# The first quad of an attention made inside the block ahead of it

## The chip, the cores and the metric

The kernel runs on one core of a Trainium2 chip. Its engines run side by side, each through its own queue in order, and wait for one another by semaphores: TensorE (PE in the profile, its weight loads PEld), VectorE (DVE), ScalarE (ACT), GpSimd (POOL) and SyncE (SP), which issues the transfers. The metric is the time of one execution on the device in microseconds (us), the median of several runs.

## The reference

The program is a stack of four layers on x, four batches of 512 tokens of width 128, each followed by a residual sum and a layer norm:

```python
x = L0_attn_x                                   # (4, 512, 128)
x = _layernorm(x + _L0_attn_ref(x, ...))        # causal attention, 16 heads
x = _layernorm(x + _L0_ffn_ref(x, ...))         # 16 experts, top 4
x = _layernorm(x + _L1_attn_ref(x, Wq, Wk, Wv)) # 16 heads of 8, no mask
x = _layernorm(x + _L1_ffn_ref(x, ...))         # two layers: local attention, gated MLP
```

The change concerns the end of the second line and the start of the third:

```python
# experts: w is the softmax of the 4 best of 16 logits
hidden = gelu(einsum('bld,efd->blef', x, w1) + b1)
exp_out = einsum('blef,edf->bled', hidden, w2) + b2
fused = sum(w[..., None] * take_along_axis(exp_out, topi[..., None], axis=2), axis=2)
# second attention; the rotation's angle depends on the batch, not on the token
q, k, v = rope(x @ Wq.T), rope(x @ Wk.T), x @ Wv.T      # 16 heads of 8
scores = einsum('bhqd,bhkd->bhqk', q, k) / sqrt(8)
out = einsum('bhqk,bhkd->bhqd', softmax(scores), v)
```

## The kernel before

The program is written by hand for each engine. It has three blocks, one behind the other: `attention0`, `experts0` and `layers`, the last holding second attention (`attention1`) and the two local layers. Between two blocks all engines meet at a barrier, and a new block's instructions begin only when all have come. Within a block nothing but the order in the code and the semaphores sets what runs when; the profile's line numbers are those of this file. Line 2754 (`cleanup_on_exit`) stands for the ends of blocks.

**Experts.** A step is one expert and one batch; 64 steps, the last four being expert 15 with batches 0 to 3. `up` (line 1040) makes the hidden products in PSUM banks 0 to 3, ScalarE applies gelu (831) and copies a high part (826), VectorE takes the low part (904), and 12 down products (1095) follow in bank 4 or 5. VectorE multiplies by the gates (977) and adds into `xT` (980). In the last steps each batch is then finished: `turn_x` transposes `xT` (1049), `copy_x` (839) puts it into `x`, `second_moments` (878, 881) and POOL's `deviation` (775, 779) give mean and deviation, `finish_norm` (910) normalises, `turn_fin` (1056) transposes back and `copy_fin` (844) writes `xT`. Batch 0's `turn_fin` stands ahead of the last 12 down products in TensorE's queue, which is strict.

**Second attention.** Its work goes by quads: 16 quads `m`, of 4 heads of one batch, 8 units each, a unit being 128 queries or keys by 2 heads. For each quad two products (`project`, 1508: w = 0 query, w = 1 key) are made; ScalarE copies a scaled leading part (`leading`, 1292), VectorE subtracts it from a scaled product (`remain`, 1378), and both halves of the result lie in `st`. For the softmax the row maxima come first: `max_scores` (1529) and `maxima` (1387) for each unit; when a quad's 8 units are done, `shift_lead` and `shift_remain` (1396, 1400) put the maxima into two bf16 parts, `turn_shift` (1556) transposes them and `copy_shift` (1303) copies them. Then `exp_scores` makes the scores again, transposed (1540), adds the shift by a product with ones (1544), and ScalarE takes the exponentials (`exps`, 1311). `project_v` (1517) makes the values and `sums` (1568) the weighted sums. PSUM banks 0 to 5 are three pairs, used in turns; bank 6 is `o_ps`, bank 7 `m_ps`. Maxima run 11 units ahead of the exponentials (`AHEAD`): before the first exponential the opening makes three quads' products and 11 units' maxima. VectorE's `tables` (1821, 1824) belong to the first local layer and stand ahead of all that.

## Time and profile before

| what | us |
|---|---|
| median of 3 runs (lowest to highest) | 1664.57 (1659.86 to 1665.05) |
| the profiled execution: its own time | 1666.25 |
| its span, first to last instruction | 1664.5 |
| TensorE busy | 1522.5 (91%) |
| VectorE busy | 1142.5 (69%) |
| ScalarE busy | 1078.2 (65%) |
| GpSimd busy | 518.7 (31%) |

The whole span says little about one seam. The share of an engine's busy time is a mean over stages with different limits, so the seam has to be read by itself: first busy times in stretches, then the timeline in order of time. In a timeline's row a bracket gives the idle time of that engine before the row and who ended it. PEclk is TensorE's granted clock as a share of its upper level, 2.4 GHz; 0.50 is the lower level, 1.2 GHz.

### The profile page before, as it was taken

How to read it: one execution, taken by the hardware profiler on the slowest of the kernel's cores; microseconds unless marked ns; L12 is line 12 of the kernel's file. 1: busy time of each engine (PE TensorE's matmuls, PEld its weight loads, DVE VectorE, ACT ScalarE, POOL GpSimd, SP SyncE). 2: the span in 40 equal slices, each digit the busy share in tenths (PEclk: the TensorE clock that was granted, in tenths of full speed). 3: DMA queues.
4: the chain of work that ended last, by engine and by line, in shares of the span. 5: the costliest groups of instructions: out<-in, count | busy, mean ns of one | idle time of the engine just before them, and what ended most of it. 6: DMA issues, size and time to landing. Idle time of an engine off the chain costs nothing. (4 is left out here: it accounts for less than half of the span.)

```text
span 1664.5 us, 30601 instructions
## 1 busy us (share of the span) xinstructions
PE 1522.5 (91%) x10286; PEld 1044.9 (63%) x10286; DVE 1142.5 (69%) x2344; ACT 1078.2 (65%) x2475; POOL 518.7 (31%) x476
## 2 busy tenths in 40 slices
PE   7999999999979999999969999996998888899986
PEld 5777777777667888888844333333666655566664
DVE  2666666666658777777768888854777753767755
ACT  2555555555567888888836777744777754777752
POOL 1222222222232111222110000015767623776632
PEclk9999999999979999999987999967999998999999
DMA  7000000000011221222100000000000000000000
GB/s 235 2 2 0 0 0 0 0 0 0 2 50 55 77 76 64 74 76 76 38 0 1 1 1 1 1 1 1 1 1 1 1 1 1 1 1 1 1 2 26
DMA packets 18994, 36.37 MB, mean 22 GB/s; under 512 B 5764, under 2 KB 11008, under 8 KB 16704
## 3 DMA queue, kind: packets, MB, share of 16 engines
q1 hardware_dynamic: 18896, 35.09, 6.3%
q8 instruction: 58, 0.95, 0.2%
q14 instruction: 40, 0.33, 0.1%
HBM read 33.91 MB, written 1.18 MB: 21 GB/s over the span
## 5 line engine op out<-in xcount | busy, mean ns | idle before, releaser
L904 DVE TENSOR_TENSOR m_hidp<-m_hid,m_hidp 128x512 fp32r<-128x512 f32 x256 | 178.6, 724 | 76.3 <-ACT m_hidp L826 75.5
L305 ACT ACTIVATE a_prob<-ps,a_negmax 128x512 f32<-128x512 f32 (+3 forms) x256 | 133.8, 525 | 146.7 <-DVE a_negmax L381 146.7
L831 ACT ACTIVATE m_hid<-ps,pre_w 128x512 f32<-128x512 f32 x256 | 175.2, 685 | 61.8 <-PE ps L1040 61.3
L1095 PE MATMUL ps<-m_hidp,m_w2p 128*128 128x512 f32 x768 | 192.1, 399 | 0.0
L1387 DVE TENSOR_REDUCE c_sb_negmax<-ps 128x1 f32<-128x512 f32 x256 | 162.5, 683 | 38.7 <-PE ps L1529 38.5
L1040 PE MATMUL ps<-m_xp,m_w1p 128*128 128x512 f32 x768 | 188.9, 395 | 0.0
L1311 ACT ACTIVATE c_sb_pT<-ps 128x512 f32<-128x512 f32 x256 | 137.4, 601 | 73.1 <-PE ps L1544 72.2
L265 POOL TENSOR_TENSOR a_qk_r<-a_qk_c,a_qk_s 128x512 f32<-128x512 f32 x64 | 81.3, 1270 | 325.3 <-DVE a_qk_s L372 325.3
L1925 ACT ACTIVATE l_sb_prob<-ps,l_sb_negmax,l_sb_rn 128x192 f32<-128x192 f32 (+1 forms) x256 | 124.0, 494 | 77.4 <-DVE l_sb_negmax L2029 77.3
L1040 PEld LDWEIGHTS ps<-m_xp,m_w1p 128*128 128x128 f32 x768 | 144.9, 189 | 36.4 <-issue 3.0
L1095 PEld LDWEIGHTS ps<-m_hidp,m_w2p 128*128 128x128 f32 x768 | 145.5, 190 | 35.2 <-issue 0.3
L826 ACT ACTIVATE m_hidp<-m_hid 128x512 fp32r<-128x512 f32 x256 | 154.0, 630 | 0.0
L381 DVE TENSOR_REDUCE a_negmax<-ps 128x1 f32<-128x512 f32 (+3 forms) x256 | 112.9, 483 | 23.3 <-PE ps L478 23.3
L2024 DVE TENSOR_REDUCE l_sb_negraw<-ps 128x2 f32<-128x384 f32 (+1 forms) x128 | 66.2, 518 | 76.0 <-PE ps L2160 75.9
L386 DVE COPY a_probT<-ps 128x512 f32<-128x512 f32 (+3 forms) x128 | 60.9, 476 | 81.2 <-PE ps L488 81.2
L500 PEld LDWEIGHTS ps<-a_probT,a_lat 128*64 128x64 f32 x1280 | 68.2, 136 | 66.8 <-issue 61.5
L500 PE MATMUL ps<-a_probT,a_lat 128*64 128x128 f32 x1280 | 98.1, 282 | 10.2 <-issue 9.0
L478 PE MATMUL ps<-a_qkT 64*128 64x256 f32 (+3 forms) x512 | 104.6, 485 | 0.0
L1529 PE MATMUL ps<-c_sb_st 32*128 32x512 f32 x256 | 87.7, 538 | 12.1 <-ACT c_sb_pT L1311 10.4
L488 PE MATMUL ps<-keep_ident,a_prob 128*128 128x128 f32 x640 | 96.2, 281 | 0.0
L2171 PE MATMUL ps<-keep_ident,l_sb_prob 128*128 128x128 f32 x448 | 71.7, 284 | 24.1 <-ACT l_sb_prob L1925 23.7
L1844 POOL TENSOR_TENSOR c_sb_pT<-c_sb_pT,l_sb_tab_s 128x512 f32<-128x512 f32 x64 | 82.7, 1312 | 21.7 <-ACT c_sb_pT L1891 21.1
(228 smaller groups left out, 3173.1 us busy)
## 6 DMA issues: line engine op xcount, KB each, us to landing
m_gate_all<-m_gates_d SPq DMA_DIRECT2D x16, 1024.0 KB, 4.7
pre_w<-w1T SPq DMA_DIRECT2D x14, 258.0 KB, 2.7
pre_w<-w2T SPq DMA_DIRECT2D x14, 256.0 KB, 2.8
pre_wqkv<-wqkv SPq DMA_DIRECT2D x2, 768.0 KB
keep_x<-x SPq DMA_DIRECT2D x1, 1024.0 KB, 9.3
out<-keep_x SPq DMA_DIRECT2D x4, 256.0 KB, 2.3
keep_xT<-xT SPq DMA_DIRECT2D x1, 768.0 KB, 5.1
pre_m_w<-l_w SPq DMA_DIRECT2D x2, 341.0 KB
```

Source lines behind the costliest of these rows:

```text
L305: nc.scalar.activation(prob[:, u % 4, 0:width(p)], score_ps(b, p, j)[:, 0:width(p)], ACT.Exp, bias=negmax[:, u:u + 1], accum_out=den[:, b ...
L381: nc.vector.tensor_reduce(negmax[:, u:u + 1], score_ps(b, p, j)[:, 0:width(p)], AX.X, ALU.max, negate=True).then_inc(max_done, 1)
L478: nc.tensor.matmul(score_ps(b, p, j)[:, 0:width(p)], qkT[r, b % 2, 0, i * P:(i + 1) * P], qkT[r, b % 2, 1, 0:width(p)], start=False, stop= ...
L500: ins = nc.tensor.matmul(o_ps[64 * j:64 * j + 64, i * P:(i + 1) * P], lat[:, b * TPB + t, :], probT[:, j, t * P:(t + 1) * P], start=(t == ...
L826: nc.scalar.activation(hidp[:, c % 2, 0, f, :], hid[:, c % 2, f, :], ACT.Copy).then_inc(high_done, 1)
L831: nc.scalar.activation(hid[:, c % 2, f, :], ps[:, f, :], ACT.Gelu, bias=w1[:, k, FF + f:FF + f + 1]).then_inc(gelu_done, 1)
L904: nc.vector.tensor_tensor(hidp[:, c % 2, 1, f, :], hid[:, c % 2, f, :], hidp[:, c % 2, 0, f, :], ALU.subtract).then_inc(low_done, 1)
L1040: ins = nc.tensor.matmul(ps[:, f, :], w1p[:, k, a, f * P:(f + 1) * P], xp[:, b, c, :], start=(i == 0), stop=(i == 2))
L1095: ins = nc.tensor.matmul(ps[:, 4 + c % 2, :], w2p[:, k, a, f, :], hidp[:, c % 2, b, f, :], start=(f == 0 and i == 0), stop=(f == FB - 1 an ...
L1311: nc.scalar.activation(pT[:, m % 2, g + i, t, :], ps[:, pair(exp_turn(e)).start + i, :], ACT.Exp, scale=SCALE).then_inc(exp_done, 1)
L1387: nc.vector.tensor_reduce(negmax[:, m % 2, t, g + i:g + i + 1], ps[:, pair(max_turn(k)).start + i, :], AX.X, ALU.max, negate=True).then_in ...
L1925: ins = nc.scalar.activation(prob[:, k % 2, i, WIN + c.start:2 * P], ps[:, 2 + k % 2, i * KEYS + c.start:(i + 1) * KEYS], ACT.Exp, bias=ne ...
```

## The change

Inside the experts' block a class `Head` takes quad 0 of batch 0 through products, parts, maxima and shift, and quad 1 through products and parts; in `head.project(pe, m, w)` m is again the quad and w query or key. These steps stand among the finishing steps of the four batches; the shift and its copy are the block's last work. `layers` starts with quad 2's first product and units 8 to 10. The finishing steps get another order: batch 0's `turn_fin` moves behind the last 12 down products, its `finish_norm` ahead of the gate product of batch 2, and transposes go to the banks of `X_TURN` and `FIN_TURN`. Maxima in the head are one reduction over two banks instead of two. Quad 2's second product, its lead and its remainder move behind the first unit of exponentials. The buffer `st` also serves as the experts' split input `xp`. Two memsets of POOL move to the experts' start, and `tables` into the iteration m = 2 of VectorE's loop. The rest of the diff, left out here, passes names through and drops the cases m = 0.

```diff
+    xp = head.st
...
+    X_TURN = [6, 7, 4, 5]
+    FIN_TURN = [6, 7, 6, 7]
...
         nc.gpsimd.memset(ones[:, :], 1.0).then_inc(consts, 1)
+        nc.gpsimd.memset(head.shp[:, :, :, :], 0.0).then_inc(head.shp_zero, 1)
...
-            if last and c >= 1:
+            if last and c in (1, 2):
                 copy_x(c - 1)
-            if last and c >= 2:
-                copy_fin(c - 2)
...
         each_step(act, step)
-        copy_x(NB - 1)
-        copy_fin(NB - 2)
-        copy_fin(NB - 1)
+        copy_fin(0)
+        copy_x(2)
+        head.leading(act, 0, 0)
+        head.leading(act, 0, 1)
+        copy_x(3)
+        copy_fin(1)
+        head.leading(act, 1, 0)
+        copy_fin(2)
+        head.leading(act, 1, 1)
+        copy_fin(3)
+        head.copy_shift(act)
...
+            if last and c == 2:
+                finish_norm(0)
...
-            if last and c >= 2:
-                finish_norm(c - 2)
-            if last and c >= 1:
+            if last and c in (1, 2):
                 second_moments(c - 1)
         each_step(dve, step)
-        finish_norm(NB - 2)
-        second_moments(NB - 1)
-        finish_norm(NB - 1)
+        second_moments(2)
+        finish_norm(1)
+        head.remain(dve, 0, 0)
+        head.remain(dve, 0, 1)
+        second_moments(3)
+        finish_norm(2)
+        head.maxima(dve, 0)
+        head.maxima(dve, 1)
+        finish_norm(3)
+        head.remain(dve, 1, 0)
+        head.maxima(dve, 2)
+        head.maxima(dve, 3)
+        head.remain(dve, 1, 1)
+        for k in range(4, 8):
+            head.maxima(dve, k)
+        head.shift(dve)
...
-            if last and c >= 1:
+            if last and c in (1, 2):
                 turn_x(c - 1)
-            if last and c >= 2:
-                turn_fin(c - 2)
+        def first_products(w):
+            pe.wait_ge(gelu_done, FB * (STEPS - 1) + w + 1)
+            head.project(pe, 0, w)
         each_step(pe, step)
-        turn_x(NB - 1)
-        turn_fin(NB - 2)
-        turn_fin(NB - 1)
+        turn_fin(0)
+        turn_x(2)
+        pe.wait_ge(fin_ev, 1)
+        first_products(0)
+        first_products(1)
+        turn_x(3)
+        pe.wait_ge(x_ev, 3)
+        head.project(pe, 1, 0)
+        turn_fin(1)
+        pe.wait_ge(gelu_done, FB * STEPS)
+        head.max_scores(pe, 0)
+        head.max_scores(pe, 1)
+        turn_fin(2)
+        head.max_scores(pe, 2)
+        head.max_scores(pe, 3)
+        head.project(pe, 1, 1)
+        turn_fin(3)
+        for k in range(4, 8):
+            head.max_scores(pe, k)
+        head.turn_shift(pe)
...
+class Head:
...
+        self.st = sb("st", [P, 2, NB, S], F32R)
+        self.lead = sb("lead", [P, 2, S], F32R)
+        self.negmax = sb("negmax", [P, 2, TPB, 4])
+        self.shp = sb("shp", [P, TPB, 4, 32], BF16)
+        self.shT = sb("shT", [P, 2, S], BF16)
+        self.oneb = sb("oneb", [P, P], BF16)
...
+    def product(self, m, w):
+        return self.ps[:, 4 if m else w, :]
+    def bank(self, k, i):
+        return (0 if k % 2 else 2) + i
+    def project(self, pe, m, w):
+        pre = self.keep["pre"]
+        if m and w:
+            pe.wait_ge(self.st_done, 3)
+        self.nc.tensor.matmul(self.product(m, w), (pre.wq, pre.wk)[w][:, m * P:(m + 1) * P],
+                              self.keep["xT"][:, 0, :], start=True, stop=True).then_inc(self.qk_mm, 1)
+    def max_scores(self, pe, k):
+        if k == 0:
+            pe.wait_ge(self.st_done, 2)
+        for i in range(2):
+            g = 2 * (k % 2) + i
+            r = slice(32 * g, 32 * g + 32)
+            if k >= 2:
+                pe.wait_ge(self.max_done, 2 * (k - 1))
+            self.nc.tensor.matmul(self.ps[:, self.bank(k, i), :], self.st[r, 0, 0, (k // 2) * P:(k // 2 + 1) * P],
+                                  self.st[r, 1, 0, :], start=True, stop=True).then_inc(self.max_mm, 1)
...
+    def leading(self, act, m, w):
+        act.wait_ge(self.qk_mm, 2 * m + w + 1)
+        if m:
+            act.wait_ge(self.st_done, w + 1)
+        c = 2 * w * NB
+        self.nc.scalar.activation(self.lead[:, w, :], self.product(m, w), ACT.Copy,
+                                  scale=self.keep["pre"].rot[:, c:c + 1]).then_inc(self.lead_ev, 1)
+    def copy_shift(self, act):
+        act.wait_ge(self.sh_mm, 1)
+        self.nc.scalar.activation(self.shT[:, 0, :], self.shT_ps, ACT.Copy).then_inc(self.sh_ev, 1)
+    def remain(self, dve, m, w):
+        dve.wait_ge(self.lead_ev, 2 * m + w + 1)
+        c = (2 * w + 1) * NB
+        self.nc.vector.scalar_tensor_tensor(self.st[:, w, m, :], self.product(m, w), self.keep["pre"].rot[:, c:c + 1],
+                                            self.lead[:, w, :], ALU.mult, ALU.subtract).then_inc(self.st_done, 1)
+    def maxima(self, dve, k):
+        g = 2 * (k % 2)
+        dve.wait_ge(self.max_mm, 2 * k + 2)
+        self.nc.vector.tensor_reduce(self.negmax[:, 0, k // 2, g:g + 2],
+                                     self.ps[:, self.bank(k, 0):self.bank(k, 0) + 2, :], AX.X, ALU.max, negate=True
+                                     ).then_inc(self.max_done, 2)
+    def shift(self, dve):
+        dve.wait_ge(self.max_done, 16)
+        dve.wait_ge(self.shp_zero, 1)
+        self.nc.vector.tensor_copy(self.shp[:, :, :, 0], self.negmax[:, 0, :, :]).then_inc(self.sh_step, 1)
+        dve.wait_ge(self.sh_step, 1)
+        self.nc.vector.tensor_tensor(self.shp[:, :, :, 1], self.negmax[:, 0, :, :], self.shp[:, :, :, 0], ALU.subtract
+                                     ).then_inc(self.sh_step, 1)
...
-        nc.gpsimd.memset(oneb[:, :], 1.0).then_inc(ones_set, 1)
-        nc.gpsimd.memset(shp[:, :, :, :], 0.0).then_inc(shp_zero, 1)
...
-        leading(0, 0)
-        leading(0, 1)
-        leading(1, 0)
-        leading(1, 1)
         leading(2, 0)
-        leading(2, 1)
-        copy_shift(0)
         for m in range(NQ):
             e = m * NUNIT
             exps(e)
             if m == 0:
+                leading(2, 1)
                 copy_v(0)
             elif m + 2 < NQ:
                 leading(m + 2, 1)
...
-        remain(0, 0)
-        remain(0, 1)
-        maxima(0)
-        maxima(1)
-        remain(1, 0)
-        maxima(2)
-        maxima(3)
-        remain(1, 1)
-        maxima(4)
-        maxima(5)
+        maxima(8)
         remain(2, 0)
-        maxima(6)
-        maxima(7)
-        shift_lead(0)
-        remain(2, 1)
-        shift_remain(0)
-        for k in range(8, AHEAD):
-            maxima(k)
+        maxima(9)
+        maxima(10)
         for m in range(NQ - 1):
             k = m * NUNIT + AHEAD
             maxima(k)
+            if m == 0:
+                remain(2, 1)
             maxima(k + 1)
             if m and m + 2 < NQ:
                 remain(m + 2, 1)
+            if m == 2:
+                tables()
             maxima(k + 2)
             maxima(k + 3)
...
-        project(0, 0)
-        project(0, 1)
-        pe.wait_ge(ones_set, 1)
-        max_scores(0)
-        max_scores(1)
-        project(1, 0)
-        max_scores(2)
-        max_scores(3)
-        project(1, 1)
-        max_scores(4)
-        max_scores(5)
         project(2, 0)
-        max_scores(6)
-        max_scores(7)
-        project(2, 1)
-        max_scores(8)
-        max_scores(9)
-        turn_shift(0)
-        max_scores(10)
+        for k in range(NUNIT, AHEAD):
+            max_scores(k)
         for m in range(NQ):
             for r in range(NUNIT):
                 e = m * NUNIT + r
                 exp_scores(e)
                 if e + AHEAD < ALL:
                     max_scores(e + AHEAD)
+                if m == 0 and r == 0:
+                    project(2, 1)
                 if m == 0 and r < NB:
                     project_v(r)
...
-        locals_[0].tables(nc.vector)
-        local[0].first(*att.vector(dve, local[0]))
+        local[0].first(*att.vector(dve, local[0], lambda: locals_[0].tables(nc.vector)))
...
-        for phase in (attention0, experts0):
-            run(phase, io, keep)
-        keep["x3"] = tile("x3", [P, NT, D])
-        run(layers, io, keep, out)
+        run(attention0, io, keep)
+        with nc.cleanup_on_exit(), ExitStack() as shared:
+            keep["head"] = Head(nc, shared, keep)
+            run(experts0, io, keep)
+            keep["x3"] = shared.enter_context(nc.sbuf_tensor("keep_x3", [P, NT, D], F32))
+            layers(nc, shared, io, keep, out)
```

TensorE, from the last 12 down products (1095 before, 1119 after) to the block's end; `keep_xT` and `keep_x` are the rows of `turn_x` and `turn_fin`, 1199 is `head.project`, 1210 `head.max_scores`. Before:

```order
L1049 MATMUL ps<-keep_ident,keep_xT 128x128 x4
L1056 MATMUL ps<-keep_ident,keep_x 128x128 x4
L1095 MATMUL ps<-m_hidp,m_w2p 128x512 x12
L1049 MATMUL ps<-keep_ident,keep_xT 128x128 x4
L1056 MATMUL ps<-keep_ident,keep_x 128x128 x4
L1049 MATMUL ps<-keep_ident,keep_xT 128x128 x4
L1056 MATMUL ps<-keep_ident,keep_x 128x128 x8
```

After:

```order
L1071 MATMUL ps<-keep_ident,keep_xT 128x128 x4
L1119 MATMUL ps<-m_hidp,m_w2p 128x512 x12
L1080 MATMUL ps<-keep_ident,keep_x 128x128 x4
L1071 MATMUL ps<-keep_ident,keep_xT 128x128 x4
L1199 MATMUL ps<-keep_xT,pre_wq 128x512
L1199 MATMUL ps<-keep_xT,pre_wk 128x512
L1071 MATMUL ps<-keep_ident,keep_xT 128x128 x4
L1199 MATMUL ps<-keep_xT,pre_wq 128x512
L1080 MATMUL ps<-keep_ident,keep_x 128x128 x4
L1210 MATMUL ps<-c_sb_st 128x512 x4
L1080 MATMUL ps<-keep_ident,keep_x 128x128 x4
```

The down products stand one turn earlier, and products and scores lie between the turns behind them.

VectorE at the same place, from the last gate product (977 before, 990 after): 1237 is `head.remain`, 1243 `head.maxima`. Before:

```order
L977 TENSOR_TENSOR m_gated<-ps,m_gate_all 128x512
L980 TENSOR_TENSOR keep_xT<-keep_xT,m_gated 128x512
L910 TENSOR_SCALAR keep_x<-keep_x,m_mv,m_rstd 128x128 x4
L878 BN_STATS m_stats<-keep_x 128x6 x4
L881 BN_AGGR m_mv<-m_stats 128x2 x4
L910 TENSOR_SCALAR keep_x<-keep_x,m_mv,m_rstd 128x128 x4
L878 BN_STATS m_stats<-keep_x 128x6 x4
L881 BN_AGGR m_mv<-m_stats 128x2 x4
L910 TENSOR_SCALAR keep_x<-keep_x,m_mv,m_rstd 128x128 x4
```

After:

```order
L921 TENSOR_SCALAR keep_x<-keep_x,m_mv,m_rstd 128x128 x4
L1237 SCALAR_TENSOR_TENSOR c_sb_st<-ps,pre_rot,c_sb_lead 128x512 x2
L889 BN_STATS m_stats<-keep_x 128x6 x4
L892 BN_AGGR m_mv<-m_stats 128x2 x4
L921 TENSOR_SCALAR keep_x<-keep_x,m_mv,m_rstd 128x128 x4
L1243 TENSOR_REDUCE c_sb_negmax<-ps 128x2 x2
L921 TENSOR_SCALAR keep_x<-keep_x,m_mv,m_rstd 128x128 x4
L1237 SCALAR_TENSOR_TENSOR c_sb_st<-ps,pre_rot,c_sb_lead 128x512
L1243 TENSOR_REDUCE c_sb_negmax<-ps 128x2 x2
L1237 SCALAR_TENSOR_TENSOR c_sb_st<-ps,pre_rot,c_sb_lead 128x512
L1243 TENSOR_REDUCE c_sb_negmax<-ps 128x2 x4
L1250 CAST c_sb_shp<-c_sb_negmax 128x16
```

Remainders and maxima lie between and behind the normalisations of batches 1, 2 and 3.

TensorE in the new block, up to the second exponentials' scores; 1508 and 1618 are `project`, 1529 and 1639 `max_scores`, 1540 and 1650 with 1544 and 1654 `exp_scores`, 1517 and 1627 `project_v`. Before, the last rows of the opening:

```order
L1556 MATMUL ps<-pre_identb,c_sb_shp 128x128 x4
L1529 MATMUL ps<-c_sb_st 128x512 x2
L1540 MATMUL ps<-c_sb_st 128x512 x2
L1544 MATMUL ps<-c_sb_shT,c_sb_oneb 128x512 x2
L1529 MATMUL ps<-c_sb_st 128x512 x2
L1517 MATMUL ps<-pre_wv,keep_xT 128x128 x4
L1540 MATMUL ps<-c_sb_st 128x512 x2
```

After, the first rows of the block:

```order
L1618 MATMUL ps<-keep_xT,pre_wq 128x512
L1639 MATMUL ps<-c_sb_st 128x512 x6
L1650 MATMUL ps<-c_sb_st 128x512 x2
L1654 MATMUL ps<-c_sb_shT,c_sb_oneb 128x512 x2
L1639 MATMUL ps<-c_sb_st 128x512 x2
L1618 MATMUL ps<-keep_xT,pre_wk 128x512
L1627 MATMUL ps<-pre_wv,keep_xT 128x128 x4
L1650 MATMUL ps<-c_sb_st 128x512 x2
```

One product and six score matmuls now stand ahead of the first exponential scores, and one product has come between the first and the second.

## Rows read from the trace of the kernel before

**Rows 1.** Busy time by stretch: us, then PE, PEld, DVE, ACT, POOL, PEclk, DMA.
```profile
864.84:887.33 22.49, 17.11 (x44) 6.03 (x44) 18.46 (x33) 6.01 (x9) 2.81 (x9) 0.58 0.00 1
887.33:1075.00 187.67, 173.50 (x1182) 68.91 (x1182) 155.84 (x281) 139.47 (x260) 8.36 (x25) 0.96 0.00 1
```

**Rows 2.** Timeline, experts' last steps: start us, us, engine, work [idle before <-releaser].
```profile
841.14 2.97 PE L1095 MATMUL ps<-m_hidp,m_w2p 128*128 128x512 f32 x12
...
843.39 1.29 DVE L904 TENSOR_TENSOR m_hidp<-m_hid,m_hidp 128x512 fp32r<-128x512 f32 x2 [0.40 <-ACT m_hidp L826]
...
844.61 0.68 DVE L977 TENSOR_TENSOR m_gated<-ps,m_gate_all 128x512 f32<-128x512 f32 x1
...
845.93 1.11 DVE L910 TENSOR_SCALAR keep_x<-keep_x,m_mv,m_rstd 128x128 f32<-128x128 f32 x4
846.96 0.86 DVE L878 BATCH_NORM_STATS2 m_stats<-keep_x 128x6 f32<-128x128 f32 x4
...
847.10 0.80 PE L1056 MATMUL ps<-keep_ident,keep_x 128*128 128x128 f32 x4 [2.55 <-DVE keep_x L910]
...
847.55 4.57 PE L1095 MATMUL ps<-m_hidp,m_w2p 128*128 128x512 f32 x12
847.86 0.38 DVE L881 BATCH_NORM_AGGREGATE m_mv<-m_stats 128x2 f32<-128x6 f32 x4
...
848.60 1.01 POOL L779 TENSOR_TENSOR m_rstd<-m_var,m_neg_half 128x4 f32<-128x4 f32 x1
...
863.23 0.60 ACT L844 ACTIVATE keep_xT<-ps 128x512 f32<-128x512 f32 x1 [3.11 <-PE ps L1056]
```

**Rows 3.** Timeline, opening of second attention.
```profile
864.85 2.04 PE L1508 MATMUL ps<-keep_xT,pre_wq 128*128 128x512 f32 x2 [1.66 <-PEq L2754]
...
867.65 0.75 DVE L1378 SCALAR_TENSOR_TENSOR c_sb_st<-ps,pre_rot,c_sb_lead 128x512 fp32r<-128x512 f32 x1 [1.32 <-ACT c_sb_lead L1292]
...
870.50 2.48 DVE L1387 TENSOR_REDUCE c_sb_negmax<-ps 128x1 f32<-128x512 f32 x4 [0.65 <-PE ps L1529]
...
884.48 0.22 DVE L1400 TENSOR_TENSOR c_sb_shp<-c_sb_negmax,c_sb_shp 128x16 bf16<-128x16 f32 x1
...
886.01 1.28 ACT L1311 ACT_TABLE_LOAD   x1
...
886.05 0.80 PE L1540 MATMUL ps<-c_sb_st 32*128 32x512 f32 x2
...
887.33 1.08 ACT L1311 ACTIVATE c_sb_pT<-ps 128x512 f32<-128x512 f32 x2
...
887.83 2.08 PE L1517 MATMUL ps<-pre_wv,keep_xT 128*128 128x128 f32 x8
...
891.11 1.08 ACT L1311 ACTIVATE c_sb_pT<-ps 128x512 f32<-128x512 f32 x2 [0.58 <-PE ps L1544]
```

**Rows 4.** A reduction's own instructions: duration ns min/median/max, first and last start.
```profile
L2015 DVE TENSOR_REDUCE l_sb_ssq<-c_sb_pT x32: 1187/1212/1214, 1131.5 to 1586.4; 128x16 f32<-128x1024 f32 x32
```

**Rows 5.** Timeline of POOL, head of the experts' block and of the next.
```profile
463.51 0.20 POOL L775 TENSOR_TENSOR m_var<-m_mv,m_eps 128x4 f32<-128x4 f32 x1 [0.38 <-DVE m_mv L881]
...
866.10 0.52 POOL L1233 MEMSET c_sb_shp<- 128x512 bf16 x1
```

**Rows 6.** Timeline of DVE in the loop, and busy time as in rows 1.
```profile
921.89 1.29 DVE L1387 TENSOR_REDUCE c_sb_negmax<-ps 128x1 f32<-128x512 f32 x2 [0.83 <-PE ps L1529]
...
945.83 1.29 DVE L1387 TENSOR_REDUCE c_sb_negmax<-ps 128x1 f32<-128x512 f32 x2 [1.56 <-PE ps L1529]
...
944.00:946.00 2.00, 2.00 (x11) 0.65 (x14) 0.44 (x2) 0.18 (x1) 0.00 (x0) 0.50 0.04 8
```

**Rows 7.** By microsecond, PE alone: us, PE busy (x), PEclk, DMA.
```profile
868.00:869.00 1.00, 0.34 (x1) 1.00 0.00 0
...
871.00:872.00 1.00, 1.00 (x6) 0.69 0.00 0
...
891.00:892.00 1.00, 1.00 (x7) 0.57 0.00 0
```

More of the change, by code:

```diff
@@ L616, in experts0 @@
     ps = keep["ps"]
+    head = keep["head"]
     pre = keep["pre"]
@@ new lines, in _, with __init__, sb, sem @@
+        first_products(0)
[16 more added lines that the diff above has]
+class Head:
+    def __init__(self, nc, ctx, keep):
+        self.nc, self.keep, self.ps = nc, keep, keep["ps"]
+        def sb(name, shape, dt=F32):
+            return ctx.enter_context(nc.sbuf_tensor("c_sb_" + name, shape, dt))
+        def sem(name):
+            return nc.alloc_semaphore("c_" + name)
+        self.st = sb("st", [P, 2, NB, S], F32R)
[4 more added lines that the diff above has]
+        self.oneb = sb("oneb", [P, P], BF16)
+        self.shp_zero = sem("shp_zero")
+        self.ones_set = sem("ones_set")
+        self.qk_mm = sem("qk_mm")
+        self.lead_ev = sem("lead_ev")
+        self.st_done = sem("st_done")
+        self.max_mm = sem("max_mm")
+        self.max_done = sem("max_done")
+        self.sh_step = sem("sh_step")
+        self.sh_mm = sem("sh_mm")
+        self.sh_ev = sem("sh_ev")
+        self.shT_ps = self.ps[:, 4, :].bitcast(BF16)[:, 0:S]
+    def product(self, m, w):
[18 more added lines that the diff above has]
+                                  self.st[r, 1, 0, :], start=True, stop=True).then_inc(self.max_mm, 1)
+    def turn_shift(self, pe):
+        pe.wait_ge(self.sh_step, 2)
+        pe.wait_ge(self.st_done, 4)
+        for i in range(TPB):
+            ins = self.nc.tensor.transpose(self.shT_ps[:, i * P:(i + 1) * P],
+                                           self.shp[:, i, :, :].rearrange("p g c -> p (g c)"),
+                                           self.keep["pre"].identb[:, :])
+        ins.then_inc(self.sh_mm, 1)
+    def leading(self, act, m, w):
[26 more added lines that the diff above has]
+                                     ).then_inc(self.sh_step, 1)
@@ L1287, in leading @@
             act.wait_ge(qk_mm, 2 * m + w + 1)
-            if m:
-                act.wait_ge(st_done, 2 * m + w - 1)
+            act.wait_ge(st_done, 2 * m + w - 1)
             c = 2 * w * NB + m // QUADS
-            src = o_ps if m == 0 and w == 1 else m_ps
-            nc.scalar.activation(lead[:, w, :], src, ACT.Copy, scale=rot[:, c:c + 1]).then_inc(lead_ev, 1)
+            nc.scalar.activation(lead[:, w, :], m_ps, ACT.Copy, scale=rot[:, c:c + 1]).then_inc(lead_ev, 1)
         def copy_v(b):
@@ L1376, in remain @@
             c = (2 * w + 1) * NB + m // QUADS
-            src = o_ps if m == 0 and w == 1 else m_ps
-            nc.vector.scalar_tensor_tensor(st[:, w, m % 4, :], src, rot[:, c:c + 1], lead[:, w, :],
+            nc.vector.scalar_tensor_tensor(st[:, w, m % 4, :], m_ps, rot[:, c:c + 1], lead[:, w, :],
                                            ALU.mult, ALU.subtract).then_inc(st_done, 1)
```

51 lines of the change are left out of this document (17 added, 34 removed).

## The prediction

> **What bounds the kernel now.** I read first the busy time by stretch. The place of the change is one seam of the program: from 837.69 to 864.84 the last steps of the experts' block, from 864.84 to 887.33 the opening of second attention, behind it its loop. In the opening TensorE is busy 17.1 of 22.5 us, but at a mean granted clock of 0.58, and ScalarE only 6.0 us; in the loop TensorE is busy 173.5 of 187.7 us at clock 0.96 [rows 1]. So the loop is bound by TensorE, while the opening is latency: nothing that the loop's exponentials need exists before 887.33. Then I read the timeline of both stretches, and looked for what ended each idle time.
>
> In the experts' tail TensorE waits 2.55 us for the normalised x of batch 0 before it may start the last 12 down products; these then take 4.57 us, where the 12 of the step before took 2.97 [rows 2]. The block's last instruction, the copy of the last turned batch, ends at 863.83, and the next block's first product starts at 864.85 [rows 2, 3]: a crossing costs 1.0 us. Behind it the chain is product, lead, remainder, scores, maxima, shift, copy of the shift, first exponential at 887.33, second at 891.11 [rows 3].
>
> **The experts' tail in the changed kernel.** The turn of batch 0 no longer stands ahead of the last 12 down products. They wait for the last low parts, which end at 844.68; TensorE is free at 844.55 (847.10 less 2.55). So they run from 844.7 to 847.7 at 2.97 us, not to 852.12: 4.4 us earlier [rows 2]. That gap is what pays for the work put in.
>
> From 844.68 on VectorE has the longest queue; I add it up at the pitch of back-to-back rows. Four normalisations: 845.93 to 846.96 is 1.03 each, 4.1. Three sets of moments, 846.96 to 848.24: 3.8. Two pairs of gate and add, 0.69 each: 2.8 [rows 2]. Four remainders of 0.75: 3.0. Eight maxima, now over two banks in one instruction: two separate ones cost half of 2.48, that is 1.24 each pair, 9.9 in all. Cast and difference of the shift: 0.45 [rows 3]. Sum 24.1. One reduction of 1024 elements takes 1.21 in another stage [rows 4], so joining two gives back 0.03 each, 0.2 in all, which I leave out.
>
> The Trainium skill, "VectorE: DVE Perf Modes", section "The TRN2 errata", charges every instruction that reads PSUM 120 cycles beside its elements; by it joining saves 0.125 us each, 1.0 us in all, and the sum would be 0.8 us less. The rows of this case decide against most of that: single reductions follow each other at 0.62, where the page's formula gives 0.66.
>
> To the 24.1 come waits. The moments of batch 2 wait for a turn and its copy: 0.2. The second remainder of quad 1 and the maxima behind it wait for a product of up to 2.04 and a turn, against 2.5 us of other maxima in the queue: I take 1.0; at the low clock everywhere it is 3, at full clock 0. POOL's deviation takes 1.4 behind its moments (848.24 to 849.61), and each time over 1 us of other VectorE work now lies between, so it stays hidden [rows 2]. VectorE is done at 844.7 + 25.3 = 870.0. Turn and copy of the shift take 1.3 (884.70 to 886.01 [rows 3]), the crossing 1.0: the new block's first product starts at 872.3, which is 7.5 us later than now. Bounds: 870.5 to 875.
>
> **The opening.** What is removed is 22.5 us up to the first exponential and 26.3 to the second. What is left: one product, 2.04, to 874.3; the scores of unit 8 and their maxima, 0.8 + 1.24, to 876.4; scores for the exponential, 1.28 from start to the exponential (886.05 to 887.33), so 877.7 for the first [rows 3]. The table load of 1.28 [rows 3] stands behind one lead on ScalarE, is over by about 876.5 and stays hidden; if the scores came a microsecond earlier it would be the limit. The second exponential stands behind what has moved between the two: scores of unit 11 (they wait until 878.3 for the maxima of unit 9, since a remainder stands ahead), 0.8; the second product of quad 2, 2.04; the first value product, 2.08; again 1.28. At the low clock that gives 884.5, 6.6 us before 891.11. With TensorE at its upper level from about 875 on, these halve and I get 881.9, 9.2 before. The trace has both: in the present opening the clock is at its upper level from 868, 3 us after the products began, and falls again between 871 and 872; the next rise comes only between 891 and 892 [rows 7]. In the changed block TensorE waits less than 1 us at a time. I take 8.0 us between these ends.
>
> **Small edits.** Two memsets move into the head of the experts' block on POOL; that of the shift takes 0.52, with the other 0.6. POOL has 0.38 of idle time there before the first deviation [rows 5], and everything in the block's head stands behind that deviation; I charge 0.3, bounds 0 to 0.6. The three table instructions (1.4 us on VectorE, free of charge in the present opening, since VectorE waits there for ScalarE anyhow [rows 3]) now stand in quad 2 of the loop, just ahead of maxima behind which VectorE has 0.83 of idle time [rows 6]; maxima of the next unit are late by 0.6, and their bank is wanted about a microsecond later. I charge 0.2, bounds 0 to 1.4. The experts' input parts and the head's parts now share one buffer; the last up products are done before the first remainder is written, so it makes no wait. No DMA is added, and POOL's fill of the value buffer ends before the first value copy.
>
> **Sum.** 8.0 - 0.3 - 0.2 = 7.5 us. The profiled execution took 1666.25 us (span 1664.5 and 1.75 around it), so 1658.75 by its own time; the median of the runs is 1.68 lower. I predict 1657.0.
>
> **Rivals.**
> *The clock is up early.* TensorE works without a long pause from 844.7 to about 853, so all of the tail's products may run at the upper level, and so may the new opening. Then VectorE ends at 869.0, the second exponential comes at 880.9, 10.2 us early: 1654.5 with the small edits. For it: the wait of 2.55 us that stands ahead of the slow down products is gone [rows 2]. Against it: in the tail's last 8 us TensorE has little to do, and the present opening fell back to the low level three microseconds after its rise [rows 7]. The Trainium skill, "TensorE: Matmul & The Clock Gate", section "What's actually happening", says that the level follows recent activity and that the point of its change varies from run to run, since the monitor isn't tied to the kernel's start. By that rule this case and the forecast can both occur in runs of one program; the rows 7 agree so far as they show rises and falls behind work and pauses.
>
> *The tail takes what the opening gives.* VectorE's queue is strict: one late product stops all behind it. If quad 1's products run at 2.04 and its leads wait in ScalarE's queue behind the copies, about 3 us come on top of the tail, and with the low clock in the opening 3.6 us of gain remain: 1661. For it: the present opening has just such pauses, as the 1.32 us in which VectorE waits for the first lead [rows 3]. Against it: eight maxima and two normalisations now lie between those steps.
>
> *Slower.* The loop is bound by TensorE, so its clock is worth more than the opening. From 944 to 946 the clock stood at its lower level, and VectorE then idled 1.56 us; that is the most that such a dip costs [rows 6]. If the shifted start made five dips more, the gain of 7.5 is gone; with eight the kernel is 5 us slower than the median, 1669.5. That would bring the loop's mean clock from 0.96 to about 0.90. For it: only that the level has dipped there before. Against: the loop's order is untouched and leaves TensorE few pauses.
>
> *It does nothing*: exponentials begin earlier, but the loop then waits for maxima, since only 8 units are ahead and not 11 when the block begins. Units 8 to 10 are made before the second exponential, though, so the lead is whole again: 1664.5, little chance.
>
> **Chances.** Forecast 0.50 (its own range 1655 to 1660), clock early 0.17, tail longer 0.22, slower 0.06, nothing 0.05. 0.3% is 5.0 us, about what a measurement of this kernel tells from no change; the three runs of before spread over 5.2. Faster by more than that: nearly all of the first two and a third of the third less what the spread takes, 0.68; within it 0.26; slower 0.06. The range from 1650.5 to 1664 leaves out the slower case and half of nothing.
>
> **What would show it.** Right: the last 12 down products start by 845 and take 3 us; the last VectorE instruction of the experts' block ends near 870 and the next block's first product starts near 872; the first exponential comes 5 to 6 us behind that, the second near 883; the loop from the second exponential to the end as long as now. Wrong: VectorE idle for over 2 us in the tail, the first exponential waiting for its table, a new idle time ahead of the first up products, or a loop whose mean clock is below 0.93.

## The result, and the profile after

The changed kernel takes 1654.94 us (median of 6 runs, 1649.97 to 1663.98), the kernel before 1664.64 (6 runs, 1659.86 to 1665.06). The ratio is 0.9954, 95% interval 0.9935 to 0.9974: 7.7 us faster, from 4.3 to 10.8. That is the difference of the means (1663.36 and 1655.71); the medians differ by 9.7. The forecast was 1657.0 in a range from 1650.5 to 1664. The profiled execution of the changed kernel took 1660.43 us with a span of 1658.7, one of the longer of its runs; its span is 5.8 us shorter than that of before.

The experts' tail in the changed kernel's timeline; the columns are those of [rows 2]:

```profile
833.80 0.69 DVE L990 TENSOR_TENSOR m_gated<-ps,m_gate_all 128x512 f32<-128x512 f32 x1
...
845.59 3.07 PE L1119 MATMUL ps<-m_hidp,m_w2p 128*128 128x512 f32 x12 [0.19 <-DVE m_hidp L915]
...
849.78 1.13 PE L1199 MATMUL ps<-keep_xT,pre_wq 128*128 128x512 f32 x2 [0.25 <-ACT keep_xT L849]
...
856.00 2.35 DVE L1243 TENSOR_REDUCE c_sb_negmax<-ps 128x2 f32<-128x1024 f32 x2
...
860.09 2.07 PE L1199 MATMUL ps<-keep_xT,pre_wk 128*128 128x512 f32 x2 [1.12 <-DVE c_sb_st L1237]
...
862.92 0.75 DVE L1237 SCALAR_TENSOR_TENSOR c_sb_st<-ps,pre_rot,c_sb_lead 128x512 fp32r<-128x512 f32 x1 [0.62 <-ACT c_sb_lead L1227]
...
863.88 4.62 DVE L1243 TENSOR_REDUCE c_sb_negmax<-ps 128x2 f32<-128x1024 f32 x4 [0.21 <-PE ps L1210]
...
868.77 0.23 DVE L1252 TENSOR_TENSOR c_sb_shp<-c_sb_negmax,c_sb_shp 128x16 bf16<-128x16 f32 x1
```

The 2.55 us in which TensorE waited ahead of the last 12 down products is gone, and they take 3.07 instead of 4.57 [rows 2]. From there VectorE is idle only where the brackets stand, 0.62 and 0.21, and for some hundredths between rows. Its queue sets the end of the block.

The opening behind it, against [rows 3]:

```profile
871.32 2.04 PE L1618 MATMUL ps<-keep_xT,pre_wq 128*128 128x512 f32 x2 [1.66 <-PEq L2847]
...
874.11 1.28 ACT L1441 ACT_TABLE_LOAD   x1
...
876.30 1.08 ACT L1441 ACTIVATE c_sb_pT<-ps 128x512 f32<-128x512 f32 x2 [0.92 <-PE ps L1654]
...
878.04 2.08 PE L1618 MATMUL ps<-keep_xT,pre_wk 128*128 128x512 f32 x2
...
882.90 1.08 ACT L1441 ACTIVATE c_sb_pT<-ps 128x512 f32<-128x512 f32 x2 [0.44 <-PE ps L1654]
```

The second exponential comes at 882.90, 8.2 us earlier than before. The same seam in busy times, columns as in [rows 1]; the last row is the loop, from the second exponential to the last cast of maxima:

```profile
845.59:858.00 12.41, 9.31 (x44) 5.87 (x44) 12.24 (x44) 5.16 (x9) 3.64 (x6) 1.00 0.00 1
859.00:882.00 23.00, 16.07 (x46) 7.57 (x46) 15.45 (x23) 5.76 (x9) 2.24 (x7) 0.50 0.00 1
...
882.90:1097.36 214.46, 199.55 (x1329) 76.48 (x1329) 174.80 (x315) 154.70 (x289) 9.22 (x28) 0.94 0.00 1
```

TensorE has its upper level (2.4 GHz) in the first half of the tail and its lower one (1.2 GHz) in the second half and in the whole opening. The same stretch of the loop before:

```profile
891.11:1102.38 211.27, 196.67 (x1329) 0.95 0.00 1
```

(here TensorE alone: us, busy, PEclk, DMA). The loop got 3.2 us longer with the same 1329 matmuls; 2.9 of that is TensorE's busy time (199.55 against 196.67). What follows the last cast takes 561.3 us instead of 562.1. So 8.2 - 3.2 + 0.8 = 5.8, the difference of the spans.

Two stretches ahead of the change differ too. The experts' block starts 1.1 us earlier (461.04 against 462.14), but the gate product of step 60 comes at 833.80 against 833.01: the block's 64 steps lost 1.9 us. The comparisons below are therefore made from that gate product, which lies just ahead of the changed tail. From there the second exponential comes after 58.10 us before and 49.10 after: 9.0 earlier.

### The profile page after: what moved, and what is told of

Same layout as the page of the kernel before. It is cut to its first block and busy times, and to the rows that moved or that the text cites. A ratio compares the mean times of both kernels' runs of the same rounds, so it can differ in the third digit from the quotient of the medians.

```text
span 1658.7 us, 30602 instructions
## 1 busy us (share of the span) xinstructions
PE 1523.9 (92%) x10286; PEld 1044.6 (63%) x10286; DVE 1142.7 (69%) x2336; ACT 1078.0 (65%) x2475; POOL 517.0 (31%) x476
## 5 line engine op out<-in xcount | busy, mean ns | idle before, releaser
L1064 PE MATMUL ps<-c_sb_st,m_w1p 128*128 128x512 f32 x768 | 192.3, 400 | 0.0
L1511 DVE TENSOR_REDUCE c_sb_negmax<-ps 128x1 f32<-128x512 f32 x240 | 152.8, 684 | 42.2 <-PE ps L1639 42.1
L1064 PEld LDWEIGHTS ps<-c_sb_st,m_w1p 128*128 128x128 f32 x768 | 145.7, 190 | 37.8 <-issue 3.0
L500 PE MATMUL ps<-a_probT,a_lat 128*64 128x128 f32 x1280 | 98.2, 282 | 10.2 <-issue 9.0
L1639 PE MATMUL ps<-c_sb_st 32*128 32x512 f32 x240 | 83.9, 527 | 10.4 <-ACT c_sb_pT L1441 10.4
```

Of the source, the lines that this page charges most:

```text
L500: ins = nc.tensor.matmul(o_ps[64 * j:64 * j + 64, i * P:(i + 1) * P], lat[:, b * TPB + t, :], probT[:, j, t * P:(t + 1) * P], start=(t == ...
L1064: ins = nc.tensor.matmul(ps[:, f, :], w1p[:, k, a, f * P:(f + 1) * P], xp[:, b, c, :], start=(i == 0), stop=(i == 2))
L1511: nc.vector.tensor_reduce(negmax[:, m % 2, t, g + i:g + i + 1], ps[:, pair(max_turn(k)).start + i, :], AX.X, ALU.max, negate=True).then_in ...
```

## The experiments

Each kernel differs from one of the two by the edit shown. "Own buffer" means the changed kernel with `xp` in a buffer of its own; e2 and e5 to e10 have it. In e6 and e8 the loop holds one product more, which was moved into it. The table gathers what the profiles say: the time of one of the experts' steps, the last down products and the second exponential counted from the gate product of step 60, the length of the loop as above, and TensorE's time at its lower level in it (summed over windows of 1 us as 2 x (1 - PEclk)).

| kernel | step us | last down | 2nd exp | loop us | at lower level | ratio of runs [95%] |
|---|---|---|---|---|---|---|
| before | 5.573 | 14.54 | 58.10 | 211.27 | 20.5 | 1 |
| after | 5.603 | 11.79 | 49.10 | 214.46 | 27.3 | 0.9954 [0.9935, 0.9974] |
| e1_order_only | 5.573 | 11.72 | 51.63 | 211.30 | 20.9 | 0.9969 [0.9955, 0.9984] |
| e2_own_xp | 5.573 | 11.73 | 48.94 | 210.81 | 17.8 | 0.9940 [0.9920, 0.9959] |
| e9_own_again | 5.573 | 11.73 | 48.45 | 217.46 | 34.1 | 0.9955 [0.9940, 0.9970] |
| e3_pad | 5.573 | 11.71 | 48.90 | 210.81 | 17.7 | 0.9960 [0.9942, 0.9977] |
| e11_pad128 | 5.573 | 11.72 | 48.29 | 212.12 | 20.5 | one run |
| e12_pad4096 | 5.603 | 11.79 | 49.08 | 210.84 | 17.0 | one run |
| e4_old_turn | 5.603 | 14.56 | 51.18 | 213.02 | 23.9 | 0.9989 [0.9976, 1.0002] |
| e5_warm | 5.573 | as e2 | 44.31 | 220.61 | 41.0 | 0.9938 [0.9917, 0.9959] |
| e10_warm_again | 5.573 | as e2 | 46.89 | 211.66 | 20.8 | 0.9946 [0.9926, 0.9965] |
| e6_late | 5.573 | 11.72 | 47.46 | 213.03 | 21.8 | 0.9948 [0.9927, 0.9969] |
| e8_both | 5.573 | as e2 | 43.68 | 216.59 | 29.7 | 0.9936 [0.9914, 0.9958] |
| e7_tables | 5.573 | 11.73 | 48.90 | 214.08 | 27.3 | 0.9943 [0.9927, 0.9960] |

("As e2": the dummy products make one group with the down products in these timelines.)

**The new order of the tail alone.** The kernel before, with the banks and the order of turns, copies and norms of the changed one, and nothing else.

```diff
+    X_TURN = [6, 7, 4, 5]
+    FIN_TURN = [6, 7, 6, 7]
...
+            if last and c == 2:
+                finish_norm(0)
...
         each_step(pe, step)
+        turn_fin(0)
+        turn_x(2)
```

> The kernel before with the new order of turns in the experts' tail alone; second attention opens as before. Theory A (the order is most of it): without the head's work VectorE's queue in the tail is short, so the block should end about 6 to 7.5 us earlier than before (863.83 to about 857), the second exponential come as much earlier, and the time fall by 6 to 7 us, to about 0.996 of before; the head then adds only about 2 us. Theory B (the earlier down products are all that the order gives): 4.4 us, the rest of the 9 us at the second exponential is the head's. In both, the experts' steps keep their 5.57 us.

Its timeline (TensorE, then ScalarE):

```profile
843.41 3.07 PE L1100 MATMUL ps<-m_hidp,m_w2p 128*128 128x512 f32 x12 [0.22 <-DVE m_hidp L907]
...
856.95 2.04 PE L1514 MATMUL ps<-keep_xT,pre_wq 128*128 128x512 f32 x2 [1.66 <-PEq L2760]
...
879.53 1.09 ACT L1317 ACTIVATE c_sb_pT<-ps 128x512 f32<-128x512 f32 x2
...
883.32 1.09 ACT L1317 ACTIVATE c_sb_pT<-ps 128x512 f32<-128x512 f32 x2 [0.58 <-PE ps L1550]
```

From the gate product of step 60 the second exponential comes 6.5 us earlier than before; the head inside the experts' block adds 2.5 to that. The loop and what follows it are as long as before. The runs agree: a median of 1659.57 us (12 runs) against 1665.64 (31 runs), 5.2 us by the ratio, of the 7.7 of the whole change. So theory A holds in the profile; by the ratio alone, whose interval goes from 2.7 to 7.5 us, A and B can't be told apart. Most of the gain is the order of the tail: 2.8 us from the earlier start of the down products, 1.5 from their shorter time, and 2.2 from what stands behind them. The head's share shows only in the profiles, since the intervals of e1 and of the changed kernel overlap.

**The turn of batch 0 back in its old place.** The changed kernel with `turn_fin(0)` ahead of the last down products and `finish_norm(0)` behind the gate and add of batch 2.

```diff
             if last and c in (1, 2):
                 turn_x(c - 1)
+            if last and c == 2:
+                turn_fin(0)
...
         each_step(pe, step)
-        turn_fin(0)
```

> The changed kernel with batch 0's last transpose put back ahead of the last 12 down products, and its normalisation back behind the accumulation of batch 2; the head stays. Theory A (VectorE's queue sets the tail): the down products come 2.5 to 4.4 us later, VectorE idles about as long before the last gate product, and all behind it shifts: block end and second exponential 2.5 to 4 us later than in the changed kernel. Theory B (the tail has slack): under 1 us.

```profile
842.45 0.66 PE L1080 MATMUL ps<-keep_ident,keep_x 128*128 128x128 f32 x4 [2.54 <-DVE keep_x L921]
...
842.87 3.04 PE L1119 MATMUL ps<-m_hidp,m_w2p 128*128 128x512 f32 x12
```

The wait is back with nearly its old size (2.54 against 2.55 in [rows 2]), and the down products start 2.8 us later by the table, but run at the upper level. Of the delay 2.1 us reach the second exponential, a little less than theory A's 2.5 and well above theory B's 1. So the wait is real and most of it is on the path. The 1.5 us for slow down products did not come back with it: they belong to the clock, which this profile found at its upper level.

The runs say more than the profile. By the ratios putting the turn back costs 5.8 us (0.9989 against 0.9954, and the intervals don't overlap); by the profile the kernel should be about 5 us faster than before, and by the ratio it is 1.8. This gap isn't explained: the one profile is of the kernel's fastest run (1653.37 us against a median of 1662.70), in which the stage ahead of the experts was 5.5 us shorter than in the changed kernel's.

**A buffer of its own for the experts' split input, and paddings.** In the changed kernel `xp` is the buffer `st` of the head. The first edit gives it an own one, the others leave it there and move the buffers behind the head by 8832, 128 or 4096 bytes per partition.

```diff
-    xp = head.st
+    xp = sb("xp", [P, 2, NB, S], F32R)
```
```diff
         self.oneb = sb("oneb", [P, P], BF16)
+        self.pad = sb("pad", [P, 2208])     # e3; 32 in e11, 1024 in e12
```

> The changed kernel, but the experts' split input gets a buffer of its own again, not the one shared with the head. In the changed kernel's trace a step of the experts takes 5.60 us, before 5.57; 12 up products take 2.80 instead of 2.76. Theory A (sharing or place of that buffer): the up products go back to 2.76 and a step to 5.57, and the block is 1.9 us shorter. Theory B (the shift of all the other buffers by the head's 24 KB per partition): nothing changes, or something else does.

> The changed kernel with one unused buffer of 8832 bytes per partition behind the head's, so that all buffers allocated after them lie 32768 bytes further than they would without the head, and not 23936. Theory A (the place of the input buffer alone): steps stay at 5.60 us. Theory B (the weights and hidden buffers lie at an unlucky offset): steps go back to 5.57 us, 1.9 us over 64 steps.

> The changed kernel with 128 bytes per partition of unused space behind the attention's shared buffers, so that later buffers lie 128 bytes further. If a fine alignment of the later buffers makes the experts' step slower, the step is 5.573 us as before; if a coarse distance between buffers does, it stays 5.603.

> The same with 4096 bytes of unused space. A fine alignment as the cause: the step stays 5.603 us, since 4096 leaves every fine alignment as it is; a coarse distance: 5.573, or something in between.

The up products between 500 and 820 us (busy us, mean ns of one), in the kernel before, the changed one, with 128 and with 4096 bytes:

```profile
L1040 PE MATMUL ps<-m_xp,m_w1p 128*128 128x512 f32 x684 | 166.8, 392 | 0.0
```
```profile
L1064 PE MATMUL ps<-c_sb_st,m_w1p 128*128 128x512 f32 x684 | 169.1, 396 | 0.0
```
```profile
L1064 PE MATMUL ps<-c_sb_st,m_w1p 128*128 128x512 f32 x685 | 167.1, 393 | 0.0
```
```profile
L1064 PE MATMUL ps<-c_sb_st,m_w1p 128*128 128x512 f32 x684 | 169.1, 396 | 0.0
```

The same matmuls take 3 to 4 ns longer each where `xp` and the other buffers stand in one relation, and 128 bytes set it right while 4096 do nothing. By the shapes in the code the changed kernel moved the experts' weights by 23936 bytes (93.5 times 256), and the buffers behind the place that `xp` had by 7552 (29.5 times 256), but not `xp` with them. An own buffer moves along, and 128 or 8832 bytes (34.5 times 256) more make the distance a whole multiple again; 4096 don't. So what the four runs fit is a fine alignment of `xp` against another buffer, and neither the sharing nor a coarse distance. Which other buffer isn't tried. It costs 0.03 us per step, 1.9 us in 64 steps. The times of whole runs are too spread to show that: with the slow step 0.9954, without it 0.9940, 0.9955 and 0.9960. That the repair is worth its 1.9 us in the median isn't shown.

**TensorE kept busy in the tail, and work moved out of the opening.** Own buffer; in e5 dummy products in bank 5 stand between the tail's real ones, behind a wait until the last copy has read that bank, and nothing reads their results. There are 30 of them (the trace has 798 products with `w2p`, that of e2 768), not the 27 that the expectations name; in e6 quad 2's second product, lead and remainder stand behind the third unit of exponentials; e8 has both.

```diff
+        def warm(n):
+            for i in range(n):
+                nc.tensor.matmul(ps[:, 5, :], w2p[:, 1, 0, i % FB, :], hidp[:, 1, 0, i % FB, :],
+                                 start=True, stop=True)
...
             head.max_scores(pe, k)
+            if k >= 5:
+                warm(4)
```
```diff
-                if m == 0 and r == 0:
+                if m == 0 and r == 2:
                     project(2, 1)
```

> The changed kernel with a buffer of its own for the experts' input (as e2), and with 27 extra products of 0.24 us, results unused, in TensorE's pauses of the tail from 854.5 to the block's end. Theory A (the low clock in the opening is paid for): the clock stays at its upper level through the tail and into the new block; the products of 2.04 us take 1.1, the second exponential comes 3 to 4 us earlier against the last experts' steps than in e2 (48.9 us behind the gate product of step 60), the time falls by as much. Theory B (VectorE sets the tail and the opening): the clock is up, but the gain is under 1 us, since TensorE's products were hidden. Theory C: the extra products delay the real ones and the tail gets longer by 1 us or more.

> As e2, with quad 2's second product, its lead and its remainder behind the third unit of exponentials and not behind the first. Theory A (this product stands on the way to the second exponential): the second exponential comes 2.0 us after where TensorE is still at the low clock, so the gap from first to second falls from 6.7 to about 4.7 us, and as the product then runs at the upper clock about 0.9 us of the time are gained. Theory B (the maxima of units 9 and 10 set the second exponential): no gap shorter than 6 us and no gain.

> e5 and e6 together. If the clock is up when the new block opens, the late product has less left to gain (2.0 us become 1.0 in either place), so I expect e5's time or up to 0.5 us less; if e5 brings nothing, e6's time.

In this profile of e5 TensorE's granted clock (us, PE busy, PEclk, DMA) is at the upper level through tail and opening, and falls in the loop:

```profile
850.00:867.00 17.00, 14.38 (x63) 1.00 0.00 1
867.00:881.00 14.00, 12.61 (x74) 1.00 0.00 0
...
896.00:906.00 10.00, 10.00 (x52) 0.66 0.01 2
```

The next fence is ScalarE in the same execution:

```profile
868.79 1.28 ACT L1455 ACT_TABLE_LOAD   x1
870.39 1.09 ACT L1455 ACTIVATE c_sb_pT<-ps 128x512 f32<-128x512 f32 x2 [0.32 <-PE ps L1668]
...
874.84 1.09 ACT L1455 ACTIVATE c_sb_pT<-ps 128x512 f32<-128x512 f32 x2
```

The second exponential comes 4.6 us earlier than in e2, more than theory A's 3 to 4, as the clock-up-early rival had it. But its loop is 9.8 us longer, and the execution is among the slowest of its kernel (1661.84 us against a median of 1654.31). e8 gained 5.3 in the opening and lost 5.8 in the loop, e6 gained 1.5 and lost 2.2; part of both losses is the moved product itself, 1.12 us in e6. In e6 the gap from the first to the second exponential falls from 6.7 to 5.0 us, so the product did stand on that way (theory A), but the runs show no gain: medians of 1656.57 us in e6 and 1654.36 in e2, 1655.01 in e8 and 1654.31 in e5. The Trainium skill, "TensorE: Matmul & The Clock Gate", section "What's actually happening", says that the clock follows recent activity and that the point of its change varies from run to run; the next two runs ask whether the loss in the loop belongs to the edit or to the execution.

**The two again.** e9 is e2's kernel, e10 is e5's; both ran on another chip than the first pair.

> The kernel with its own input buffer once more, beside the one with dummy products. Theory (time at TensorE's lower level moves from the opening into the loop, where it costs more): the second exponential 48.9 us after the gate product of step 60, the last maxima cast some 210 to 214 us behind it, lower level mostly ahead of the loop; median within 2 us of the dummy kernel's. Rival (the dips of the loop fall by chance of the execution): this profile may show 217 or more from the second exponential to the last cast, as the dummy kernel's first profile did (220.6).

> The kernel with own buffer and 27 dummy products once more. Theory: the second exponential again 44 to 45 us after the gate product of step 60 (4.6 earlier), but 216 us or more from there to the last cast, because the loop meets more of the lower level; the median no more than 2 us from the kernel without dummies. Rival (chance): 211 to 213 us to the last cast, and then the median 3 to 4 us lower than without dummies.

The rival holds, and so the traces agree with the page that the level's changes fall differently from run to run. The loop in e2 and e9 (no dummies), then in e5 and e10 (dummies):

```profile
882.03:1092.84 210.81, 195.81 (x1329) 0.96 0.00 1
```
```profile
881.68:1099.14 217.46, 202.61 (x1329) 0.92 0.00 1
```
```profile
874.84:1095.45 220.61, 205.75 (x1329) 0.91 0.00 1
```
```profile
880.27:1091.93 211.66, 196.68 (x1329) 0.95 0.00 1
```

The kernel without dummies had 210.81 us in one execution and 217.46 in the other, that with dummies 220.61 and 211.66. So my theory that time at the lower level is pushed from the opening into the loop falls: the amount in the loop varies from one execution to the next, whatever the edit. It isn't the chip either: the nine runs of e5 on one chip range from 1651.52 to 1662.98 us, the two slowest with a mean granted clock of 0.963 and 0.962, the others with 0.968 to 0.971. What holds in all 14 rows of the table is that the loop's length less half of its time at the lower level is 200.1 to 202.3 us, and that TensorE is idle in the loop for 14.6 to 15.0 us: the differences lie in its busy time. The dummies don't hold the clock in every execution either; e10's row for the stretch that was at 1.00 in e5 is

```profile
867.00:881.00 14.00, 11.68 (x45) 0.76 0.00 0
```

and its second exponential comes only 1.6 us earlier than in e9. As to the time: in the first pair the medians are 1654.36 without dummies and 1654.31 with, in the second 1658.32 and 1654.87, which is the 3 to 4 us that the rival foresaw. All runs together have 1655.12 (20 runs) and 1654.46 (15 runs), and the ratios differ by 0.0002 and 0.0009, well inside their intervals. So a gain in time from the dummies is neither shown nor excluded.

**The tables back at the head of the new block.** Own buffer, `tables` ahead of the first maxima.

```diff
+        tables()
         maxima(8)
...
-            if m == 2:
-                tables()
```

> As e2, with the three table instructions of VectorE at the new block's head, where VectorE waits 2.7 us for the first scores, and not in iteration 2 of the loop. Theory A (they cost 0.2 us in the loop, since VectorE has slack there): within 0.5 us of e2 from the second to the fifth shift of the loop. Theory B (VectorE sets the loop): 1.4 us less there than in e2.

Where they stand in the changed kernel (VectorE):

```profile
914.28 0.68 DVE L1915 TENSOR_TENSOR l_sb_tab_c<-pre_base_c,pre_qks 128x512 f32<-128x512 f32 x1
914.88 0.75 DVE L1918 TENSOR_TENSOR l_sb_tab_s<-pre_base_s,pre_qks 128x256 f32<-128x256 f32 x2
```

In e7 they run at 870.92 and hold up nothing: the first exponential comes 4.98 us behind the block's first product, as in the changed kernel. In e2 they run at 910.72, in the loop. What the expectation compares, the time from the second to the fifth shift, fits neither theory: 45.32 us in e7 and 42.59 in e2, 2.7 more without the tables in the loop. That is the clock again, since e7's loop has 27.3 us at the lower level and e2's 17.8. TensorE's idle time in that quad tells more. Its wait for VectorE ahead of the next product, in e2 and then in e7:

```profile
915.10 1.10 PE L1618 MATMUL ps<-keep_xT,pre_wq 128*128 128x512 f32 x2 [0.72 <-DVE c_sb_att L1531]
```
```profile
919.12 1.10 PE L1617 MATMUL ps<-keep_xT,pre_wq 128*128 128x512 f32 x2 [0.36 <-DVE c_sb_att L1531]
```

The kernel before has the 0.36 too. Over the whole loop TensorE is idle for 14.6 us in the three kernels with the tables at the head (before, e1, e7) and for 14.9 to 15.0 in the other eleven. So in the loop they cost 0.3 to 0.4 us, and at the head nothing; the ratios (0.9943 and 0.9940) can't show so little.

## Why the prediction was right

*Down products.* Forecast 844.7 with 2.97 us; measured 845.59 with 3.07. Of the 0.9 us of lateness 0.8 is the later gate product of step 60 (the slower steps, less the earlier start of the block); counted from the gate product of step 60 the edit brings 2.8 us of start and 1.5 of duration, 4.3 against the forecast's 4.4. e1 shows the same start, and e4 shows that the wait comes back with the old turn. That the edit gave the 1.5 us of duration isn't shown: in e4 the down products wait as before and still take 3.04 us.

*VectorE's queue.* Forecast 25.3 us from the start of the down products to its end, measured 23.4 (845.59 to 869.00). The waits were 0.8 instead of 1.2, and the terms of the queue were sized too long: eight joined maxima took 2.35 + 2.35 + 4.62 = 9.3 us, not 9.9, and the moments, gates, adds and remainders come to 0.7 less than charged. Four single reductions take 2.48 us [rows 3] and two joined ones 2.35, so joining gives back 0.065 us each, more than the 0.03 I had read from a reduction of another stage [rows 4], and less than the 0.125 of the Trainium skill's formula ("VectorE: DVE Perf Modes", section "The TRN2 errata").

*The new block.* Forecast at 872.3, measured at 871.32, or 870.5 without the late experts; that is the lower bound given. The first exponential follows after 4.98 us (forecast 5.4), with the table load hidden, since it ends at 875.39. The second follows after 6.60, where the low-clock row gave 6.8. So the second exponential's gain of 8.2 us (9.0 from the gate product on) agrees with the 8.0 that was charged, but by errors that cancel: VectorE's queue was 1.9 us shorter than thought, while its start was 0.9 late, and the opening ran wholly at the lower level, where I had put the value between both levels, which cost 0.8. The reason given for the upper level, that TensorE waits less than 1 us at a time there, was met (its longest wait is 0.45 us between 871.32 and 882.90), and the clock stayed at 0.50 all the same.

*Small edits.* The two memsets:

```profile
461.20 0.53 POOL L791 MEMSET c_sb_shp<- 128x512 bf16 x1
461.67 0.20 POOL L792 MEMSET c_sb_oneb<- 128x128 bf16 x1
...
462.49 0.20 POOL L778 TENSOR_TENSOR m_var<-m_mv,m_eps 128x4 f32<-128x4 f32 x1
```

The first deviation starts 1.45 us behind the block's first moments (461.04), before 1.37 (463.51 in [rows 5], 462.14): 0.08, not 0.3. POOL's idle 0.38 took part of them. The tables cost 0.3 to 0.4 where 0.2 was charged, as e7 shows.

*What was missed.* The buffers' placement. I wrote that the shared buffer makes no wait, which is true, and took that for no cost; the step of 5.603 us instead of 5.573 is 1.9 us in the profile, a quarter of the gain.

*Sum and rivals.* Forecast 7.5 us, measured 7.7 by the ratio, 9.7 by the medians and 5.8 by the spans of the two profiles. That one of these lies within 0.2 of the forecast is luck: the interval is 6.5 us wide, and the loop, which was to be as long as before, got 3.2 longer in the profile. "Clock up early" occurred in half of the tail but not in the opening; e5 forced it there and reached 44.31 us. "The tail takes it" did not occur (0.83 us of waits). "Nothing" is excluded by the interval. "Slower" had the right mechanism, but its price for a dip, the 1.56 us that VectorE idled [rows 6], was the wrong one: the loops lose half of the time that TensorE spends at its lower level. Between executions the loop holds 17.0 to 41.0 us at the lower level, which is 12 us of time, more than the whole gain. But this goes with the execution and not with the edit, as e2 with e9 and e5 with e10 show; how far the loop of the kernel before varies, its one profile doesn't tell. A second source is the stage ahead of the experts: in the 14 profiles the experts' block starts between 455.56 and 462.40. The forecast came out right for the kernel's runs taken together; that these average both sources out is argued, and one profile against another would not have shown it. Two small slips of the sums changed nothing: 10.2 less the small edits' 0.5 gives 1654.9 for the early clock, not 1654.5, and eight joins at 0.125 take 1.0 off the 24.1, not 0.8.

## What to carry to other kernels

Where an engine works its queue in order, look for the one instruction that waits for another engine ahead of work that is ready. Putting it back cost 2.1 us in the profile and 5.8 by the ratios; the new order of the whole tail, of which this move is a part, gave 6.5 of the 9.0 us, and the head in it the rest. When a buffer is shared or added, compare the time of one matmul of the untouched loops before and after: here a shift of 128 bytes was worth 1.9 us by the step times. And before a gain of a few microseconds is put down to an edit, compare two profiles of one and the same kernel, since a stage can differ by more than that between its executions.

## What the runs showed of the hardware

- The placement of buffers in SBUF changed the rate of matmuls. The up products' mean is 396 ns instead of 392, and the experts' step 5.603 instead of 5.573 us. 128 bytes more restore it (393 ns), 4096 bytes don't (396 ns), 8832 bytes do (392 ns).
- Two executions of one program differed by 6.6 us (e2 and e9) and by 9.0 us (e5 and e10) in one and the same loop, with TensorE at its lower level for 17.8 against 34.1 us, and 41.0 against 20.8. The difference lies in its busy time (195.81 against 202.61, 205.75 against 196.68); its idle time in the loop stays between 14.6 and 15.0 us in all profiles.
- Dummy products held TensorE at its upper level through a tail and an opening in e5 (17 and 14 us at 1.00), where real work alone had left it at 0.50 from 859 to 882 us in the changed kernel. In a second execution of the same kernel (e10) the opening's 14 us had only 0.76.
- Joining two reductions of 512 elements from PSUM into one of 1024 saved 0.065 us: four single ones take 2.48 us, two joined ones 2.35.
